# Products of key and value formed in token rows, and transposes that put them one token further, in the scan of a recurrent layer

## What is computed

```python
w = jnp.exp(-jnp.exp(time_decay + jnp.tanh(x5[:, :, 1] @ decay_w1) @ decay_w2))
r = (x5[:, :, 3] @ Wr.T).reshape(b, l, H, S)
k = (x5[:, :, 0] @ Wk.T).reshape(b, l, H, S)
v = (x5[:, :, 2] @ Wv.T).reshape(b, l, H, S)
g = jax.nn.silu(x5[:, :, 4] @ Wg.T)

def step(s, rkvw):
    r_t, k_t, v_t, w_t = rkvw
    a = k_t[:, :, :, None] * v_t[:, :, None, :]
    out = jnp.einsum('bhk,bhkd->bhd', r_t, u * a + s)
    return (a + w_t[:, :, :, None] * s, out)
```

## Time and profile before

| | |
|---|---|
| time, median of 3 runs | 1250.8 us (1249.71 to 1253.63) |
| the profiled execution | 1254.03 us, span 1252.2 us |
| TensorE (PE) busy | 1112.4 us, 89% |
| VectorE (DVE) busy | 861.2 us, 69% |
| ScalarE (ACT) busy | 541.8 us, 43% |
| GpSimd (POOL) busy | 424.9 us, 34% |
| mean granted TensorE clock | 0.962 of 2.4 GHz |
| last layer | from 919.9 us to the end |

### The profile page before, as it was taken

How to read it: one execution, slowest core, us unless ns; L and a number is a source line. 1 busy time by engine, 2 the same in 40 slices (tenths; PEclk the granted TensorE clock), 3 DMA queues, 4 the chain that set the end, 5 groups by cost and what they waited for, 6 DMA issues and landing times. The chain is left out here.

```text
span 1252.2 us, 21156 instructions
## 1 busy us (share of the span) xinstructions
PE 1112.4 (89%) x7808; PEld 694.3 (55%) x7808; DVE 861.2 (69%) x1605; ACT 541.8 (43%) x1004; POOL 424.9 (34%) x387
## 2 busy tenths in 40 slices
PE   6977878899999999999999999888988988989966
PEld 4654556558658657658667667564442432523414
DVE  4875776776866865866866866854467696595664
ACT  3535344464473463474474473441304314314221
POOL 2111343343332442342343343332235254164240
PEclk9998888999999999999999999989998997999988
DMA  7120100000102002102100000120010010000100
GB/s 235 59 93 18 44 1 18 22 2 20 36 0 67 21 0 76 34 0 70 51 14 19 21 17 17 53 79 17 1 34 20 1 38 16 6 30 1 34 0 17
DMA packets 37375, 40.73 MB, mean 33 GB/s; under 512 B 8064, under 2 KB 32832, under 8 KB 37072
## 3 DMA queue, kind: packets, MB, share of 16 engines
q1 hardware_dynamic: 37200, 40.01, 10.0%
q0 software_dynamic: 128, 0.10, 0.1%
HBM read 31.71 MB, written 8.39 MB: 32 GB/s over the span
## 5 line engine op out<-in xcount | busy, mean ns | idle before, releaser
L1329 DVE TENSOR_REDUCE b_neg_max<-head_area 128x16 f32<-128x1024 f32 x64 | 77.9, 1217 | 87.2 <-POOL head_area L764 86.7
L2034 POOL TENSOR_TENSOR c_rs<-c_st,head_area 128x512 f32<-128x512 f32 x64 | 82.2, 1286 | 129.9 <-DVE c_st L2442 129.9
L769 POOL TENSOR_TENSOR b_rstd<-b_var,minus_half 128x1 f32<-128x1 f32 x63 | 34.5, 548 | 256.8 <-DVE b_var L1358 256.8
L1012 PE MATMUL ps<-b_hT_mlp,wl 128*128 128x512 f32 x224 | 108.8, 608 | 8.4 <-ACT b_hT_mlp L1145 7.2
L1180 ACT ACTIVATE head_area<-head_area 128x1024 f32<-128x1024 f32 x64 | 68.0, 1062 | 103.3 <-DVE head_area L1334 102.7
L1026 PE MATMUL ps<-w,b_act_g 128*128 128x256 f32 x448 | 105.7, 390 | 2.7 <-ACT b_act_g L1198 2.7
L764 POOL TENSOR_TENSOR head_area<-head_area,b_self_add 128x1024 f32<-128x1024 f32 x32 | 75.7, 2365 | 81.0 <-DVE head_area L1322 81.0
L764 POOL TENSOR_TENSOR head_area<-head_area,b_cross_add 128x1024 f32<-128x1024 f32 x32 | 75.4, 2358 | 80.6 <-DVE head_area L1322 80.6
L1185 ACT ACTIVATE head_area<-ps 128x512 f32<-128x512 f32 x128 | 70.2, 606 | 63.4 <-PE ps L960 63.4
L1026 PEld LDWEIGHTS ps<-w,b_act_g 128*128 128x128 f32 x448 | 85.0, 195 | 18.4 <-issue 4.6
L845 PE MATMUL ps<-head_area,wl 128*128 128x512 f32 x176 | 85.0, 606 | 2.0 <-SPq L661 2.0
(11 more groups left out here) (251 smaller groups left out, 2336.9 us busy)
## 6 DMA issues: line engine op xcount, KB each, us to landing
b_x_in<-x_mid SPq DMA_DIRECT2D x9, 512.0 KB, 3.9
wl<-in_wl SPq DMA_DIRECT2D x4, 1024.0 KB, 6.7
head_area<-in_ctxT SPq DMA_DIRECT2D x8, 512.0 KB, 3.8
x_mid<-b_x_out SPq DMA_DIRECT2D x8, 512.0 KB, 2.9
area<-in_wc SPq DMA_DIRECT2D x1, 2336.0 KB, 8.3
a_x_in<-in_x SPq DMA_DIRECT2D x16, 128.0 KB, 2.8
a_y_in<-in_ctx SPq DMA_DIRECT2D x16, 128.0 KB, 3.4
w<-in_w SPq DMA_DIRECT2D x2, 1024.0 KB, 9.5
```

Source lines behind the costliest of these rows:

```text
L1012: mm = pe.matmul(ps[:, YB + j % 2, :], weight("w1", k, j * P, (j + 1) * P), hT_mlp[:, k, :], start=(k == 0), stop=(k == NC - 1))
L1329: dve.tensor_reduce(neg_max[:, k % 2, :], t, AX, ALU.max, negate=True).then_inc(max_ok, 1)
L2034: pool.tensor_tensor(rs[:, i % 4, :], st[:, i % 3, :], rF[:, i // RS, :], ALU.mult).then_inc(rs_ok, 1)
```

## The change

The product of key and value is formed with tokens on partitions, and TensorE's transposes bring it into the banks of the scan.

- k and v are copied out of PSUM without padding (`kF`, `vF`). `to_tokens` transposes them back into token rows: per matrix and chunk four transposes of 128x128 into a `PROJ` bank, then one copy by ScalarE (`copy_tokens`) into `k_tok` or `v_tok`. It stands behind mix_pair(8) (k) and behind norm_T (v) in a turn, and behind hidden(6) and mix_pair(8) in the first head.
- `key_value` multiplies, on VectorE and from SBUF to SBUF, one tile of 128 tokens by 16 heads x 8 keys x 8 values: 128x1024, four for a chunk. Those of chunk 0 stand in the turn between ffn_mix and own_weight; those of chunk 1 in the recurrence behind scans 0, 1, 2 and 3.
- `update` takes the place of `spread_v`: four transposes of 128x128 of `kv` with the matrix `next_token` instead of the unit matrix. It moves each token on by one inside its sequence. The start state then overwrites column 0 as before. `scan` waits for the start state, not for a product.
- The padding of keys and values and two memsets are gone. Several buffers of the middle layers now share an area with those of the last layer's head.

```diff
@@ last_mlp_first_head, TensorE
+            def to_tokens(src, done, m):
+                for c in range(NC):
+                    pe.wait_ge(done, c + 1)
+                    bank_free(m + c)
+                    for p in range(NP):
+                        mm = pe.transpose(ps[:, PROJ + (m + c) % 2, p * P:(p + 1) * P], src[:, c, p * P:(p + 1) * P], w["ident"][:, :])
                     mm.then_inc(proj_ps, 1)
...
             hidden(6)
+            to_tokens(kF, k_ok, FIRST_OUT["k_tok"])
             project(2, "v")
             mix_pair(8)
+            to_tokens(vF, v_ok, FIRST_OUT["v_tok"])
             hidden(7)
@@ last_mlp_first_head, VectorE
             pre(7)
+            key_value()
             own_weight()
@@ phase_c, TensorE
-            def spread_v(n, i):
-                c = place(i)[0]
+            def update(n, i):
+                c, d = i // RS, 2 * (i % 4) + i % RS // 4
                 if i >= 4:
                     pe.wait_ge(st_ok, NS * n + i - 3)
-                pe.matmul(seqs(ps[:, VB[i % 4], :]), w["sel"][:, i % RS, :], vS[:, c, :, 0:S], start=True, stop=True).then_inc(vb_ps, 1)
+                if i % RS == 0:
+                    pe.wait_ge(kv_ok, NC * NP * n + NP * (c + 1))
+                for p in range(NP):
+                    mm = pe.transpose(ps[:, VB[i % 4], p * P:(p + 1) * P], kv[c][:, p, d * P:(d + 1) * P], w["next_token"][:, :])
+                mm.then_inc(kv_ps, 1)
...
                 if head:
                     mix_pair(n, 8)
+                    to_tokens(n, kF, k_ok, FIRST_OUT["k_tok"])
                     project(n, 2, "v")
                 if tail:
                     norm_T(1, last)
                 if head:
+                    to_tokens(n, vF, v_ok, FIRST_OUT["v_tok"])
                     project(n, 3, "r")
@@ phase_c, ScalarE
+            def copy_tokens(n, name, dst, ok):
+                for c in range(NC):
+                    m = FIRST_OUT[name] + c
+                    act.wait_ge(proj_ps, OUTS * n + m + 1)
+                    act.activation(dst[:, c, :, :].rearrange("q p f -> q (p f)"), ps[:, PROJ + m % 2, :], ACT.Copy).then_inc(ok, 1)
...
-                    copy_projection(n, lambda c: kS[:, c, :, 1:S + 1], k_ok, 1)
-                    copy_projection(n, lambda c: vS[:, c, :, 1:S + 1], v_ok, 2)
+                    copy_projection(n, "k", kF, k_ok)
+                    copy_tokens(n, "k_tok", k_tok, tok_ok)
+                    copy_projection(n, "v", vF, v_ok)
+                    copy_tokens(n, "v_tok", v_tok, tok_ok)
                 if tail:
                     norm_out(1, last, "ln2_w", "ln2_b")
@@ phase_c, VectorE
-            def key_value(n, i):
-                dve.wait_ge(s0_ok, NS * n + i + 1)
-                kv = seqs(ps[:, VB[i % 4], :])
-                dve.tensor_tensor(kv, kv, kS[:, i // RS, :, 0:S], ALU.mult).then_inc(kv_ok, 1)
+            def key_value(n, c, tiles):
+                dve.wait_ge(tok_ok, 2 * NC * n + NC + c + 1)
+                for p in tiles:
+                    key = k_tok[:, c, p, :].rearrange("q (h k) -> q h k", h=HC).unsqueeze(1).broadcast_to([P, RS, HC, RS])
+                    value = v_tok[:, c, p, :].rearrange("q (d h) -> q d h", d=RS).unsqueeze(3).broadcast_to([P, RS, HC, RS])
+                    dve.tensor_tensor(kv[c][:, p, :].rearrange("q (d h k) -> q d h k", d=RS, h=HC), key, value, ALU.mult).then_inc(kv_ok, 1)
...
                 dve.wait_ge(decay_ok, 2 * NC * (n + 1))
-                key_value(n, 0)
                 for i in range(NS):
-                    if i + 1 < NS:
-                        key_value(n, i + 1)
                     scan(n, i)
+                    if KV2[0] <= i < KV2[0] + NP:
+                        key_value(n, 1, [i - KV2[0]])
...
                 if head:
+                    key_value(n, 0, range(NP))
                     own_weight(n)
@@ kernel, the constant
-    lay["sel"] = np.stack([(i % HC == j // RS) & (i // HC == d) for d in [*range(0, RS, 2), *range(1, RS, 2)]], 1)
+    lay["next_token"] = (i // S == j // S) & ((i + 1) % S == j % S)
```

## The result

The changed kernel takes 1240.9 us (median of 6 runs, 1238.7 to 1243.8) where the kernel before, timed beside it, takes 1249.7 (1248.0 to 1253.6): a ratio of 0.9929, 95% interval 0.9906 to 0.9951. Timed again, they gave 1243.4 against 1250.6, ratio 0.9942 (0.9918 to 0.9965). So it is 7 to 9 us faster, where I had forecast 2.

The account below looks back on a forecast made before the run. VectorE was taken to bound the recurrences, TensorE and the engines feeding it the turns. Recurrences -8.8, turns +5.7, end of middle layers +1.1 sum to -2.0 us, from 1250.8 to 1248.8; range 1242.5 to 1257.

Parts of the forecast that it names:

- Recurrence, gain 2.2: The last layer's four recurrences: each 2.2 us shorter with the products between scans gone, 8.8 us in all.
- The door: Recurrence steps 0 to 3: VectorE's new product and POOL's product block each other at SBUF, VectorE's going first.
- 2.39: Recurrence steps 0 to 3: predicted us per step, 1.13 scan + 1.14 product + 0.12 for POOL's longer product.
- Rival A: Recurrences: the door costs nothing, steps 0 to 3 take 2.27 us, 5.8 us less, 1243.0; chance 0.3 with milder form.
- its milder one: Turns: half the waits for copies hide in TensorE's gaps, up to 1.2 us less per turn, 1245.2; within the 0.3.
- Turn, +1.9: Each turn between recurrences: +3.1 us for transposes and copies, -1.2 at the recurrence's start; +5.7 over three.
- Rival C: Turns: the four products reach own_weight late and push result, at most 1.8 us per turn, 1254; chance 0.05.
- Head +2.9: End of the middle layers: ScalarE's four extra copies delay the GELU, so mlp_out starts 2.9 us late.
- handover -1.8: Handover to the last layer's first scan: its wait falls from 2.8 to 1.0 us, returning 1.8.
- Rival B: Recurrences: TensorE's clock falls to 1.2 GHz; 1267 if it lasts beyond step 4, 1254.8 if short; chance 0.2.
- the forecast's band: Whole kernel: 1246 to 1251.5 us around the forecast time, chance 0.45.
- the full low clock: Rival B's full case: 1.2 GHz for whole recurrences, 33.7 us each instead of 29.1, 18 us over four, 1267; chance 0.05.

## Why the prediction was off, point by point

**Recurrence, gain 2.2: right, a little small.** It was 31.2 - 28.75 = 2.45 in three and 28.9 - 26.2 = 2.7 in the last. The door (the way to SBUF that VectorE and POOL share) is real and in the order given: VectorE's product goes first. But a step is 2.25 us, not 2.39, since POOL's product ends with the scan beside it and not 0.12 after it. Taking the products out gave 4.0 us back, and POOL's products lost 0.87 each beside them. Rival A's main form is refuted, and its milder one, which had the turns grow by up to 1.2 us less, too: they grew by 1.67 of the forecast's 1.9. That the measured 1240.9 us lies nearest to its 1243.0 is chance.

**Turn, +1.9: right.** 53.19 against 51.52 with the clock high in both, +1.67, from 2.8 in the turn and -1.1 in the handover; moving transposes and copies off the chain returned 1.54. The four products hide as I said: in the changed kernel they run from 988.67 to 993.29 and result still waits its 3.06 us, as in the earlier trace rows:

```profile
988.67 4.62 DVE L2498 TENSOR_TENSOR head_area<-head_area 128x1024 f32<-128x1024 f32 x4
...
999.03 0.42 DVE L2563 SCALAR_TENSOR_TENSOR c_ff<-c_rr,ps 128x256 f32<-128x256 f32 x1 [3.06 <-PE ps L2249]
```

Rival C did not occur.

**Head +2.9, handover -1.8: right.** TensorE reached hidden at 868.59, 3.11 us earlier than in the profile before (871.70), and mlp_out began at 900.99, behind the GELU, against 901.05: 3.05 late. The last layer's first matmul to its first scan went from 2.82 to 1.03.

```profile
897.23 3.71 ACT L1741 ACTIVATE b_act_g<-b_act_g 128x2048 f32<-128x2048 f32 x2
```

So the parts, measured, give 3 x -2.45 - 2.7 + 3 x 1.67 + 1.3 = -3.7 us. With the clock held up in both kernels the chip gives -3.5, with some 2.4 us of scatter to either side. Against the forecast's -2.0 these terms alone would have left the time near 1247 us, inside the forecast's band.

**The clock: the step that failed.** Rival B asked only what a low clock would cost the changed kernel in its recurrences. I read the low stretch of the kernel before at 950.14, named it as evidence that the clock can fall, and never priced it. I looked at that one alone, where the profile has ten low stretches from the first scan on. So the sum put at nothing, without a reason, what low clock costs the kernel before and how much of that the change moves away. The sign stood in the table by stage: 57.6 us at 0.91 are some 10 us at 1.2 GHz. The price did not: that turn took 53.7 us and one without a fall 51.5. It is a cost that the kernel before pays, and a change that shifts TensorE's load can shift it to a place where it is nearly free. Held up by extra matmuls in turns and tail, the kernel before gained 7.3 us (0.9942), and the changed one 2 to 3.5 (0.9914 against 0.9929 and 0.9942). The difference, some 4 to 5 us and known to 2 or 3, is the surplus: -3.7 - 4.5 = -8.2, against the measured -7.3 and -8.7.

I had also taken the full low clock as the danger, at 0.05. It did not come. In the first recurrence the clock rose again at 931.2, and with pairs of eight transposes and four sums from there on it stayed at 2.4 GHz to the end:

```profile
932.60:949.80 17.20, 13.48 (x71) 5.98 (x70) 16.18 (x17) 3.17 (x13) 12.65 (x10) 1.00 0.11 35
```

**What stays open.** Why the falls wander in the kernel before and stand still in the changed one isn't settled. So it is luck in part that the change moved them to a better place: nothing in the prediction or the runs says beforehand where they go, and with small edits to the changed kernel they came back into the turns. Nor is it settled why in the same kernel the layers ahead of the last differ by 4.5 us from run to run (first scan at 921.0 and 925.5 in the two profiles of the changed kernel). That scatter is in every time here, and it is larger than the effect of one small edit.

## What to carry to other kernels

A clock dip is a cost with a place. Before costing a change, list the dips of the kernel as it is, ask of each whether TensorE was the bound there, and ask where the changed load will put them. Where TensorE waits just ahead of a stage that it bounds, a few matmuls without use can pay for themselves; in a place where the dip was free the same matmuls brought nothing, and the dips came back in the turns. And a stage that gets shorter on one engine uncovers the next: products taken out of VectorE's queue were worth their price only while TensorE kept ahead of the bonus.

## What the hardware showed

Work added to TensorE made a kernel faster: five matmuls a turn and four ahead of the tail, 1250.1 to 1243.5 us. In the changed kernel a VectorE product of 128x1024 with both inputs in SBUF was never slowed by POOL's product beside it (1.20 us each time); POOL's went from 1.27 to 2.14, later by 0.87:

```profile
922.38 2.09 POOL L2068 TENSOR_TENSOR c_rs<-c_st,head_area 128x512 f32<-128x512 f32 x1 [25.78 <-DVE c_st L2506]
```

This first one starts 0.23 us behind the start of VectorE's product (922.15) and takes 0.82 us more than its 1.27. It thus came free about 0.15 us before that product's recorded end (923.35). The Trainium skill ("SBUF — State Buffer", Who interferes with whom) has the later of the two fully blocked while the other holds the port. The order and the block agree with it, but for these 0.15 us; I had let POOL wait until the recorded end, and that accounts for the 0.12 in my step.
